# Graph convolution with residual and layer norm on one core: which rows of a block a partition holds, and how the squares are read

## The reference

```
A = adj + eye(N)
deg = sum(A, axis=1)
d = rsqrt(deg)
h = (A * d[:, None] * d[None, :]) @ x
y = x + elu(h @ w)
out = (y - mean(y)) / sqrt(var(y) + 1e-5)     # over the 128 features
```

## Time and profile before

| | before |
|---|---|
| median of 3 runs | 1063.69 us |
| lowest, highest | 1060.98, 1064.75 us |
| the profiled execution | 1063.25 us |
| its span (first to last instruction) | 1061.5 us |
| mean granted TensorE clock | 0.966 of full |
| moved by DMA | 367.28 MB, mean 346 GB/s |
| DMA packets | 168809, of them 32976 under 2 KB |

### The profile page before, as it was taken

How to read it: one execution, slowest core, us unless ns; L and a number is a source line. 1 busy time by engine, 2 the same in 40 slices (tenths; PEclk the granted TensorE clock), 3 DMA queues, 4 the chain that set the end, 5 groups by cost and what they waited for, 6 DMA issues and landing times. The chain is left out here.

```text
span 1061.5 us, 35545 instructions
## 1 busy us (share of the span) xinstructions
PE 926.1 (87%) x16000; PEld 840.2 (79%) x16000; DVE 763.0 (72%) x632; ACT 703.2 (66%) x1677; POOL 194.3 (18%) x267
## 2 busy tenths in 40 slices
PE   0099299398797998999999999998999999999994
PEld 0065288287796897999998987998899999999994
DVE  0496496576587677878787867987688796866933
ACT  6898898898888888898888988860204715032201
POOL 0220120300401204040421444474001101000000
PEclk9999689799899999999999999999899999999998
DMA  9999999999999999999999999889898898999910
GB/s 384 401 387 413 399 392 403 395 399 397 399 394 385 384 384 394 335 391 393 392 395 389 395 396 383 298 283 364 271 307 277 285 327 282 306 305 313 351 73 21
DMA packets 168809, 367.28 MB, mean 346 GB/s; under 512 B 6224, under 2 KB 32976, under 8 KB 158416
## 3 DMA queue, kind: packets, MB, share of 16 engines
q1 hardware_dynamic: 151760, 356.60, 91.1%
q10 hardware_dynamic: 16896, 8.39, 2.7%
HBM read 360.78 MB, written 4.19 MB: 344 GB/s over the span
## 5 line engine op out<-in xcount | busy, mean ns | idle before, releaser
L881 PE MATMUL p_set<-space 32*128 32x256 f32 (+3 forms) x15872 | 908.7, 387 | 118.0 <-ACT space L791 56.5
L881 PEld LDWEIGHTS p_set<-space 32*128 32x128 f32 x15872 | 824.0, 188 | 198.5 <-issue 132.8
L899 DVE STREAM_TRANSPOSE space<-space 128x2048 f32<-128x2048 f32 x256 | 579.1, 2291 | 115.5 <-ACT space L783 87.4
L783 ACT ACTIVATE space<-space 128x512 f32<-128x512 f32 (+2 forms) x744 | 578.9, 779 | 82.0 <-DMA space<-in_adj 76.5
L923 DVE TENSOR_TENSOR hT<-p_set,hT 128x1024 f32<-128x1024 f32 (+2 forms) x108 | 105.8, 997 | 118.3 <-PE p_set L881 118.2
L783 ACT ACTIVATION_READ_ACCUMULATOR space<-space 128x1 f32 x744 | 138.8, 187 | 0.0
L806 ACT ACTIVATE space<-space 128x512 f32<-128x512 f32 x16 | 10.1, 631 | 190.2 <-DVE space L934 190.1
L766 POOL COPY space<-xn 32x512 f32<-32x512 f32 x192 | 119.9, 625 | 12.3
L750 POOL TENSOR_TENSOR d<-deg,half 128x4 f32<-128x4 f32 x16 | 16.3, 1017 | 540.7 <-DVE deg L905 540.7
L791 ACT ACTIVATE space<-xn 32x512 f32<-32x512 f32 x96 | 60.2, 627 | 49.0 <-POOL xn L756 43.7
L773 POOL TENSOR_TENSOR rstd<-var_eps,half 128x4 f32<-128x4 f32 x16 | 16.5, 1031 | 247.3 <-DVE var_eps L968 247.3
(11 more groups left out here) (16 smaller groups left out, 28.6 us busy)
## 6 DMA issues: line engine op xcount, KB each, us to landing
space<-in_adj SPq DMA_DIRECT2D x332, 1024.0 KB, 12.3
xn<-in_x SPq DMA_DIRECT2D x20, 256.0 KB, 11.4
space<-in_x ACTq DMA_DIRECT2D x16, 256.0 KB, 8.1
out_rows<-space ACTq DMA_DIRECT2D x16, 256.0 KB, 8.6
space<-in_adj SPq DMA_DIRECT2D x4, 768.0 KB, 12.0
ident<-in_w SPq DMA_DIRECT2D x1, 64.0 KB, 13.7
```

The source lines that it names most:

```text
L783: ins = nc.scalar.activation(view[:, g], view[:, g], ACT.Copy, accum_out=to[:, g:g + 1])
L881: ins = nc.tensor.matmul(to, xs_chunk(h, j)[quadrant(q)], moving, start=first and s == b == 0, stop=last and s == b == 3)
L899: nc.vector.transpose(slots[slot], slots[slot]).then_inc(tile_turned, 1)
```

## The change

1. **Rows to partitions.** Partition p now holds rows 4p to 4p + 3 of a block. For x, the residuals and the output, four rows of 128 features lie side by side in memory, so that a partition's 2 KB are one packet, where there were four of 512 bytes. For `adj` the pieces keep their length (2 KB of a tile row, up to 8 KB of a strip); only the order of the rows is another.
2. **Squares.** A contraction index is dealt in the same way, node 4p + b of a band on partition p: a square of 32 x 32 is made of every fourth column of a row group. The turn becomes four instructions per tile, one for each row group, of 4 x 4 squares whose elements lie four floats (16 bytes) apart in reading and in writing. TensorE's moving operand is read with the same step of four floats. The diagonal that GpSimd adds to has that step too.
3. **w** is loaded from ScalarE's queue, as an item of the plan of its own ("w", after the 16th diagonal), and SP's list loses it.
4. **The end.** The last two bands (`LAST = 2`) are normalised half by ScalarE and half by VectorE; the last product's addition is made in one instruction per band, with a semaphore step each, where it was one for both.

```diff
+LAST = 2
-W_AFTER = 8
...
+            counts["diagonals"] += 1
+            if counts["diagonals"] == BANDS:
+                offer("act", 0, "w", 0, 0.1)
...
-            last = adds[-1] if adds and adds[-1][0] == job else None
+            last = adds[-1] if adds and adds[-1][0] == job and job != last_job else None
...
-        x_rows = x.rearrange("(n b p) f -> n p b f", b=BLOCKS, p=128)
-        out_rows = out.rearrange("(n b p) f -> n p b f", b=BLOCKS, p=128)
+        x_rows = x.rearrange("(n p b) f -> n p b f", b=BLOCKS, p=128)
+        out_rows = out.rearrange("(n p b) f -> n p b f", b=BLOCKS, p=128)
...
-                return adj[BAND * u:BAND * (u + 1), BAND * t:BAND * (t + 1)].rearrange("(k p) c -> p k c", p=128)
+                return adj[BAND * u:BAND * (u + 1), BAND * t:BAND * (t + 1)].rearrange("(p k) c -> p k c", p=128)
...
-            row = BAND * r + 128 * k0
-            return adj[row:row + 128 * nk, x0:x0 + wide].rearrange("(k p) c -> p k c", p=128)
+            return adj[BAND * r:BAND * (r + 1), x0:x0 + wide].rearrange("(p k) c -> p k c", p=128)[:, k0:k0 + nk]
...
-                if what == "load" and arg == agains[W_AFTER]:
-                    sp.wait_ge(diagonal_added, BANDS)
-                    sp.dma_start(w_sb[:, :], w).then_inc(w_loaded, 16)
...
-                    on_diagonal = bass.AP(corner.tensor, corner.offset, [[BLOCKS * SLOTS * BAND, 128], [SLOTS * BAND + 128, BLOCKS], [1, 128]])
+                    on_diagonal = bass.AP(corner.tensor, corner.offset, [[BLOCKS * SLOTS * BAND, 128], [SLOTS * BAND + 1, BLOCKS], [BLOCKS, 128]])
...
-                for b in range(BLOCKS):
+                for b in range(BLOCKS) if n < BANDS - LAST else range(BLOCKS // 2):
...
+                elif kind == "w":
+                    act.wait_ge(diagonal_added, BANDS)
+                    act.dma_start(w_sb[:, :], w).then_inc(w_loaded, 16)
...
-                            chunk = space[quadrant(q), 0, at[0], 32 * j:32 * j + 32]
+                            chunk = space[quadrant(q), 0, at[0], 128 * s + b:128 * s + b + 32]
                             step = at[1] - at[0] if len(at) > 1 else 1
-                            moving = bass.AP(chunk.tensor, chunk.offset, [[BLOCKS * SLOTS * BAND, 32], [BAND * step, len(at)], [SLOTS * BAND, BLOCKS], [1, 32]])
+                            moving = bass.AP(chunk.tensor, chunk.offset, [[BLOCKS * SLOTS * BAND, 32], [BAND * step, len(at)], [SLOTS * BAND, BLOCKS], [BLOCKS, 32]])
...
-                    nc.vector.transpose(slots[slot], slots[slot]).then_inc(tile_turned, 1)
+                    for k in range(BLOCKS):
+                        squares = slots[slot][:, k].rearrange("p (s i b) -> p s b i", s=Q, b=BLOCKS)
+                        ins = nc.vector.transpose(squares, squares)
+                    ins.then_inc(tile_turned, 1)
...
-                    for b in range(BLOCKS):
+                    for b in range(BLOCKS // 2, BLOCKS):
```

More of the change, by code:

```diff
@@ L89, in plan @@
     step_left = [BANDS] * BANDS
-    counts = {"z": 0, "stored": 0, "outs": 0, "residuals": 0}
+    normed = {}
+    counts = {"diagonals": 0, "w": 0, "z": 0, "stored": 0, "outs": 0, "residuals": 0}
     at_row, row_todo, rows_done, stage_open = 0, strip_items(0, kept), False, True
@@ L113, in allowed @@
         if kind == "out":
-            return free_set() is not None and counts["residuals"] > 0 and (counts["outs"] == counts["z"] or not parts_left())
+            return free_set() is not None and counts["residuals"] > 0 and counts["w"] > 0 and (counts["outs"] == counts["z"] or not parts_left())
         if kind == "z":
@@ L357, in finished @@
             counts["residuals"] = 1
+        elif kind == "w":
+            counts["w"] = 1
         elif kind == "out":
@@ L372, in finished @@
         elif kind == "shift":
-            offer(*(("act", 1, "normalise", arg, 1.7) if arg < BANDS - 1 else ("dve", 1, "normalise", arg, 1.6)))
+            if arg < BANDS - LAST:
+                offer("act", 1, "normalise", arg, 1.7)
+            else:
+                offer("act", 1, "normalise", arg, 0.9)
+                offer("dve", 1, "normalise", arg, 0.65)
         elif kind == "normalise":
-            offer("act", 1, "store", arg, 0.5)
+            normed[arg] = normed.get(arg, 0) + 1
+            if normed[arg] == (1 if arg < BANDS - LAST else 2):
+                offer("act", 1, "store", arg, 0.5)
         elif kind == "store":
@@ L548, in gcn_resnorm @@
     adds, begun = [], {}
+    last_job = [a for k, a in order["dve"] if k == "add"][-1]
     for job in (a for k, a in order["dve"] if k == "add"):
         for i, u in enumerate(jobs[job][1]):
-            last = adds[-1] if adds and adds[-1][0] == job else None
+            last = adds[-1] if adds and adds[-1][0] == job and job != last_job else None
             if last and u == last[2] + last[3] and bool(last[4]) == (u in begun):
@@ L704, in _ @@
         def _(sp):
-            agains = [arg for what, arg in order["sp"] if what == "load" and loads[arg][:2] == ("tile", "again")]
             for what, arg in order["sp"]:
-                if what == "load" and arg == agains[W_AFTER]:
-                    sp.wait_ge(diagonal_added, BANDS)
-                    sp.dma_start(w_sb[:, :], w).then_inc(w_loaded, 16)
                 if what == "x":
@@ L818, in store @@
             def store(n):
[L820 to L823, removed]
+                act.wait_ge(normed, n + 1)
+                if n >= BANDS - LAST:
+                    act.wait_ge(last_normed, n - (BANDS - LAST) + 1)
                 if n + RING < BANDS:
```

## The result

The changed kernel takes **2004.69 us** (median of 4 runs, 2003.74 to 2004.99) against 1062.55 us before: a ratio of 1.887, 95% interval 1.884 to 1.891. I had forecast 1059.2 us, a little faster. It is 88.7% slower, and close to the heavy end of my rival 3, to which the forecast range did not reach.

A forecast was written before the change was run, and what follows sets the result against it. DMA was taken to bound the kernel up to 405 us, TensorE after. 1063.25 - 4.0 - 1.2 - 1.0 + 1.0 + 0.7 = 1058.75, forecast as 1059.2 us against the runs shown; range 1053 to 1110 us.

The forecast's parts named there:

- rival 3: TensorE reads its columns slower: 1,230 us in all at VectorE's rate, 1,950 if doubled; chance 0.10.
- What bounds the kernel: DMA up to the home at 405.64 us, then TensorE, busy 588 of 600 us from 400 to 1000.
- the step of 16 bytes: Strided access in turns and TensorE's reads: taken as costing nothing; bounds nothing, or the element time doubled.
- the fill of 64 elements: Elements 68 bytes apart take 112 ns, against 134 at twice 1.04 ns each: writing apart isn't doubled.
- Rival 2: VectorE becomes the bound: a turn takes 4.6 us at 2.09 ns per element, some 1,415 us in all; chance 0.12.
- w: Loaded from ScalarE's queue, it lands earlier and closes TensorE's gap of 3.97 us at 744.34 us: -4.0 us.
- tail: From the last addition on: addition per band, halved normalisation and last stores apart, -1.2 us.
- The diagonals: GpSimd's addition, 1.25 us for 512 elements, reads at 16-byte steps: +0.7 us, at most 3.8.
- The row order: Four rows between partitions' pieces of `adj`: taken as nothing, at most 12 us in the first 400 us.
- packets: x in 2 KB packets: 0.16 us saved per 256 KB load, six loads count in the DMA-bound stage, -1.0 us.
- four turns: Four turn instructions for one on VectorE: 0.25 us more per tile, mostly hidden, +1.0 us ahead of a home.
- The rule of the Trainium skill: SBUF lines of 16 bytes need two hits for full rate; its chance was rivals 2 and 3 together, 0.22.

The follow-up runs named there:

- e10: e1_natural with each turn split into four instructions that read contiguously and write with a step of four floats: 1260.05 us.
- e3: e1_natural with the change's four strided turns alone (step of four floats in reading and writing), TensorE reading contiguously: 1312.83 us.
- e1_natural: The change with all layout edits taken back, w on ScalarE's queue and the new tail kept: 1055.61 us, ratio 0.9959 to the kernel before.
- e4_rows: The change with contiguous turns and TensorE reads; row order, 2 KB packets and the diagonal's step stay: 1054.89 us, ratio 0.9943 to the kernel before.

## Why the prediction was wrong

- **What bounds the kernel: right**, and it is why the error was so dear. TensorE had no slack after 405 us, so its columns were a term that any factor multiplies, and in the event all 889 us of it: the matmuls of line L881 were busy 908.7 us and are busy 1853.4 as L891, +945; their waits stayed at about 120 us, and the kernel grew by 942.
- **The step that failed** is "I take nothing" for the step of 16 bytes, and in it two readings. First, "VectorE and TensorE take one 4-byte element at a time here" was taken to mean that the place of the next element doesn't matter. The runs show that an element in a line of its own takes 1.77 ns, twice a column's 0.87 and 1.7 times VectorE's 1.04. Second, the fill of 64 elements, 112 ns. I set it against 64 x 2.09 = 134 and concluded that writing apart isn't doubled, which is so for that fill. At the 1.68 ns that e10 measured for a turn's writes, its elements would take 108 ns and leave 4 for all the rest of the instruction, so this fill may well pay nothing. The other fill, 1024 elements in runs of 16 adjacent ones, shows that a fill takes at most 912 / 1024 = 0.89 ns for an element; how much of the 112 ns is fixed it doesn't show. What failed is that I carried this row over to another operation, the turn, and to reads, for which I had none. The other fill, in the view of its line L887 of the kernel before:

```profile
L887 DVE MEMSET sums<- x1: 912/912/912, 1.0 to 1.0; 128x1024 f32 x1
```

- **Rival 3** named the mechanism, TensorE reading slower, and its heavy end of 1,950 us was 2.7% below what came. Its chance of 0.10 was too small, and its worst case lay outside my range. Its reason, that TensorE asks more of SBUF than VectorE, isn't what decides: VectorE pays 1.78 ns too.
- **Rival 2** was right too, in its parts: the quarter took 1.10 us for my 1.2, and alone, in e3, the turns make 1313 us for my 1,415. The element pays 1.7 times, not twice. In the change all but 26 us of it is hidden behind rival 3. Two figures of these rivals were slightly off, to no effect: the element time at which VectorE becomes the bound is 1.26 times today's, (3.03 / 4 - 0.085) / 0.534, and not 1.29, and a fifth more on 889 us gives some 1,240 and not 1,230.
- **Small terms.** w 3.4 to 4.0 us for 4.0, tail 1.0 for 1.2 (both e1_natural). The diagonals rose by 0.3 us each, which fits the little that I took. The row order cost nothing that can be seen, as taken; packets and four turns are unresolved. The sum without the steps would have been right in direction and near in size: e4_rows and e1_natural are 0.6 and 0.4% faster, for my 0.4%.
- **The rule of the Trainium skill** (SBUF — State Buffer, Door 1: The DMA port swizzle) that each line needs two hits had 0.22 in my text and was right: 1.77 ns against 0.87. I let the sentence beside it, four fp32 as a free step, lower its chance, although the new layout then stood exactly on the edge, where the two sentences disagree.

## What to carry to other kernels

If a change makes the bounding engine read in another pattern, the price of that pattern is the whole forecast: when no row shows it, the range has to reach its worst case, or one short run must measure it first. For such matmuls and turns count the 16-byte lines that an operand enters per element, and compare about 1.8 ns per line with the engine's time per element. In these runs fp32 at a step of two cost VectorE nothing and TensorE 5%, at a step of four 1.7 times and twice. Gains of packets are to be looked for only where DMA is what is waited for: here a quarter of the packets on ScalarE's queue was worth 0.7 us by the medians of e4_rows and e1_natural, too little to be told from nothing.

## What the runs showed of the hardware that was not expected

- One figure serves two engines: 1.77 to 1.81 ns per 16-byte line in TensorE's moving reads, 1.78 in VectorE's reads, 1.68 in its writes. Reading and writing with the step cost VectorE hardly more than reading alone, 1.80 ns.
- The engines don't slow each other by it: TensorE's matmul is 625 ns with and without strided turns beside it.
- GpSimd's addition of 512 elements rose by only 0.3 us with the step, to 1575 ns in the change and 1546 in e4_rows, from 1279 in the kernel before and in e1_natural.
